# Expert affinities as fp32 products of an fp32 x^T, weights spread on VectorE, x split on GpSimd

## The chip, the core and the metric

One core of a Trainium2 chip runs the whole program. The metric is device time in microseconds (us), the median of several runs: lower is better. The engines are PE (TensorE), DVE (VectorE), ACT (ScalarE), POOL (GpSimd) and SP (the queue that issues the DMAs).

## The reference

The input is eight sequences of 512 tokens by 128 values. Three steps follow each other, each of them normalising its input over the 128 values first:

```
x = x + 0.5 * ffn(layernorm(x))          # first FFN
x = x + attn(layernorm(x))               # a gated step: two 128x128 products, a shift by one token, a sigmoid gate
x = x + 0.5 * ffn(layernorm(x))          # second FFN, same weights

def ffn(x):                              # x: tokens x 128
    shared = silu(x @ Ws_up) @ Ws_down
    aff = x @ centroids.T                # tokens x 64 experts
    idx = top_k(aff + expert_biases, 8)
    w = sigmoid(aff[idx]); w = w / (sum(w) + 1e-8)
    cw = w scattered to tokens x 64, zero elsewhere
    y = sum over experts e of cw[:, e] * (silu(x @ W_up[e]) @ W_down[e])      # 64 experts, 128 -> 64 -> 128
    return shared + y
```

All experts are computed for all tokens, and `cw` weighs them.

## The kernel before

The program works through 16 phases. A phase is one FFN of one sequence: 33 tiles of 512 tokens, tile 0 the shared expert and 32 tiles of two hidden columns of all 64 experts. Each tile has an up product into one of five PSUM banks `up`, a silu in place (ACT, L421), a product with the routing weights `cw` (DVE, L580; tile 0 has none), a split of the result into `g_hi` (fp32r, ACT, L429) and `g_lo` (the rest: even tiles DVE L589, odd tiles POOL L353), and a down product that adds into the bank `y_ps`. Up and down products are each three matmuls, hi*hi, lo*hi and hi*lo (L711 to L713). In its queue PE has the down product of tile t-6 ahead of the up product of tile t, and before tile t it waits until tile t-5 has been taken out of its bank.

Beside these tiles, at slots t given by tables (`AT_FIRST` for the first phase, `AT_SECOND`, `AT_THIRD`, then `AT_STEADY_A` and `AT_STEADY_B` in a loop of five turns, `AT_MID_PREP` and `AT_LAST`), each engine does a piece of the rest. Every engine walks the slots in the same order, so a table's number sets the place in its queue. The routing of the next phase is such a piece:

- PE turns the normalised `normed` to x^T in the PSUM bank `side1` (`x_t`, L720). ACT rounds it to `x_hi` (L408), DVE takes the rest as `x_lo` (L533).
- PE multiplies x_hi with `ce_both` (the centroids, hi and lo side by side, L731) and x_lo with the hi half (L732), four pairs, into `side1`. DVE adds the two halves to `aff` (L537), ACT takes the sigmoid (L412), DVE adds the bias (L541), finds the eight largest (L547), marks them (L554), selects (L561), sums (L566), adds 1e-8 (L570) and inverts (L574).
- POOL multiplies and doubles to `w_dup` (L347), PE turns it (L720), ACT copies it to `cw` (L416). In the first phase w_dup is made on DVE (L692).

The other pieces are the two layernorms around the attention (DVE L513, L520, L526, POOL L341, L343), the attention's products (L752 to L757) and its end on DVE: `t1` (L646) and `x2` (L656). Sigmoid and silu each load their table on ACT (1.28 us).

Before the first phase a prologue loads and norms the first sequence and goes through its routing, while PE runs fill-in products (`keep_busy`, L707). The weights come in four DMA pieces and are split hi/lo in eight pieces of each kind: hi on ACT (L478, L483), lo on DVE (L595) or POOL (L360, L367).

Of the kernel before, what the change touches and what calls it, by code (L numbers as in the profile page):

```python
# [6 lines left out]
B, T, D = 8, 512, 128  # L7
# [27 lines left out]
WARM_START, WARM_ROWS, WARM_ROUTE = 12, 4, 7  # L35
# [3 lines left out]
class Phase:  # L39
# [22 lines left out]
    "x_t": 11, "x_hi": 12, "x_lo": 12, "aff": 16, "aff_sum": 16, "sig": 18, "bias": 17, "max": 18, "take": 18,  # L62
    "gate": 20, "sum": 22, "eps": 23, "inv": 24, "cw": 25, "cw_t": 33, "cw_copy": 33,
# [24 lines left out]
    "x_t": 6, "x_hi": 7, "x_lo": 9, "aff": 12, "aff_sum": 12, "sig": 15, "bias": 13, "max": 15, "take": 15,  # L88
    "gate": 17, "sum": 20, "eps": 22, "inv": 23, "cw": 24, "cw_t": 31, "cw_copy": 32,
# [41 lines left out]
def build(nc, x, ident_in, cent_t, ebias, ws_up, ws_down, w_up, w_down, wb, wb_t, wbf, wbf_t, w1, w2, b_in, out):  # L131
# [3 lines left out]
    with ctx:  # L135
# [20 lines left out]
        ce_both = sb("ce_both", [P, 2 * E], fp32r)  # L156
# [6 lines left out]

        x_hi = [sb(f"x_hi{q}", [P, T], fp32r) for q in range(2)]
# [724 lines left out]
```

## Time and profile before

| what | value |
|---|---|
| median of 3 runs | 822.33 us (821.82 to 822.52) |
| the profiled execution | 821.78 us, its span 820.0 us |
| PE busy | 805.1 us, 98% |
| DVE, ACT, POOL busy | 692.7, 650.7, 408.3 us |
| granted TensorE clock | full in all 40 slices |

The span runs from the first to the last instruction; the 1.8 us around it belong to the time too. PE's busy time is the union of its matmuls, which overlap; how densely they follow each other is read from their starts. The DMAs matter in the first 20 us alone (slices 1 and 2: 267 and 23 GB/s).

### The profile page before, as it was taken

What the parts mean: (1) busy time and instruction counts of PE and PEld (TensorE: products, weight loads), DVE (VectorE), ACT (ScalarE), POOL (GpSimd) and SP (SyncE); (2) the same over time, 40 slices, a digit from 0 to 9 for tenths busy, and PEclk for the clock granted to TensorE, in tenths of its full rate; (3) what the DMA queues carried; (4) which work ended last, traced back from release to release, by engine and by line L of the source; (5) the groups of instructions that cost most, each with busy time, mean ns of one, the idle gap of its engine ahead of it and who ended that gap; (6) DMA issues with size and microseconds to landing.
All of it is one profiled execution on the core that took longest, in us unless ns stands there. A gap on an engine that the chain in (4) does not pass through costs nothing.

```text
span 820.0 us, 12468 instructions
## 1 busy us (share of the span) xinstructions
PE 805.1 (98%) x3691; PEld 649.5 (79%) x3691; DVE 692.7 (84%) x1451; ACT 650.7 (79%) x1204; POOL 408.3 (50%) x360
## 2 busy tenths in 40 slices
PE   7999999999999999999999999999999999999998
PEld 5778878778888788888888788887888878888786
DVE  7987989888798887988879888798897988788875
ACT  5897778778787787877878688886888868786975
POOL 2884545545455453544535445364463644554453
PEclk9999999999999999999999999999999999999999
DMA  7000000000000000000000000000000000000000
GB/s 267 23 0 14 14 1 1 1 10 17 14 1 0 21 4 13 0 0 26 0 13 0 0 26 0 13 0 0 26 0 0 0 1 27 0 1 1 14 0 14
DMA packets 16046, 11.51 MB, mean 14 GB/s; under 512 B 1680, under 2 KB 14992, under 8 KB 16016
## 3 DMA queue, kind: packets, MB, share of 16 engines
q1 hardware_dynamic: 16016, 11.15, 4.4%
q8 instruction: 15, 0.25, 0.1%
q14 instruction: 15, 0.12, 0.1%
HBM read 9.05 MB, written 2.10 MB: 14 GB/s over the span
## 4 chain that ended last, share of the span: by engine, by line
PE 77%; DVE 14%; ACT 5%; issue 1%; POOL 1%; DMA 0%; DVEq 0%; ACTq 0%; POOLq 0%
PE up L711 12%; PE up L712 12%; PE up L713 12%; PE y_ps L711 11%; PE y_ps L713 11%; PE y_ps L712 11%; PE side L720 3%; DVE x L656 3%; DVE g_lo L589 2%; DVE gated L580 2%; ACT up L421 2%; ACT g_hi L429 2%; DVE normed L526 2%; DVE up L580 2%; PE side L731 1%
## 5 line engine op out<-in xcount | busy, mean ns | idle before, releaser
L353 POOL TENSOR_TENSOR g_lo<-gated,g_hi 128x512 fp32r<-128x512 f32 x256 | 331.9, 1297 | 372.5 <-ACT g_hi L429 372.5
L421 ACT ACTIVATE up<-up 128x512 f32<-128x512 f32 x528 | 310.7, 590 | 73.6 <-PE up L713 72.1
L580 DVE TENSOR_TENSOR gated<-up,cw 128x512 f32<-128x512 f32 x256 | 175.3, 685 | 58.1 <-ACT up L421 53.9
L711 PE MATMUL y_ps<-g_hi,wd_hi 128*128 128x512 f32 x512 | 208.0, 406 | 1.8 <-POOL g_lo L353 1.7
L711 PE MATMUL up<-x_hi,wu_hi 128*128 128x512 f32 x512 | 203.1, 397 | 1.8 <-DVE g_lo L589 1.8
L713 PE MATMUL y_ps<-g_hi,wd_lo 128*128 128x512 f32 x512 | 202.5, 396 | 0.0
L712 PE MATMUL up<-x_lo,wu_hi 128*128 128x512 f32 x512 | 202.3, 395 | 0.0
L713 PE MATMUL up<-x_hi,wu_lo 128*128 128x512 f32 x512 | 201.7, 394 | 0.0
L712 PE MATMUL y_ps<-g_lo,wd_hi 128*128 128x512 f32 x512 | 201.6, 394 | 0.0
L429 ACT CAST g_hi<-up 128x512 fp32r<-128x512 f32 x272 | 161.2, 592 | 47.8 <-DVE up L580 45.8
L580 DVE TENSOR_TENSOR up<-up,cw 128x512 f32<-128x512 f32 x256 | 176.4, 689 | 18.1 <-ACT up L421 14.4
L589 DVE TENSOR_TENSOR g_lo<-up,g_hi 128x512 fp32r<-128x512 f32 x256 | 174.3, 681 | 10.6 <-ACT g_hi L429 9.3
L429 ACT CAST g_hi<-gated 128x512 fp32r<-128x512 f32 x256 | 157.4, 615 | 28.8 <-DVE gated L580 26.8
L711 PEld LDWEIGHTS up<-x_hi,wu_hi 128*128 128x128 f32 x512 | 96.3, 188 | 27.3 <-DVE g_lo L589 4.1
L711 PEld LDWEIGHTS y_ps<-g_hi,wd_hi 128*128 128x128 f32 x512 | 96.4, 188 | 25.1 <-POOL g_lo L353 4.1
L713 PEld LDWEIGHTS y_ps<-g_hi,wd_lo 128*128 128x128 f32 x512 | 96.3, 188 | 23.0
L713 PEld LDWEIGHTS up<-x_hi,wu_lo 128*128 128x128 f32 x512 | 96.3, 188 | 22.5
L712 PEld LDWEIGHTS up<-x_lo,wu_hi 128*128 128x128 f32 x512 | 96.4, 188 | 22.3
L712 PEld LDWEIGHTS y_ps<-g_lo,wd_hi 128*128 128x128 f32 x512 | 96.6, 189 | 18.7
L526 DVE TENSOR_SCALAR normed<-x,mv,rstd 128x128 f32<-128x128 f32 x64 | 35.0, 598 | 1.3 <-POOL rstd L343 1.1
L589 DVE TENSOR_TENSOR g_hi<-up,g_hi 64x512 fp32r<-64x512 f32 x16 | 11.1, 694 | 20.0 <-ACT g_hi L429 19.8
L343 POOL TENSOR_TENSOR rstd<-var_eps,neg_half 128x4 f32<-128x4 f32 x24 | 25.3, 1053 | 2.0
(101 smaller groups left out, 570.9 us busy)
## 6 DMA issues: line engine op xcount, KB each, us to landing
x_in<-in_x SPq DMA_DIRECT2D x8, 256.0 KB, 2.8
wu_raw<-in_w_up SPq DMA_DIRECT2D x4, 512.0 KB, 6.1
wd_raw<-in_w_down SPq DMA_DIRECT2D x4, 512.0 KB, 7.0
x_res<-in_x SPq DMA_DIRECT2D x8, 256.0 KB, 2.8
out<-out_sb SPq DMA_DIRECT2D x7, 256.0 KB, 2.2
out<-out_sb SPq DMA_DIRECT2D x2, 128.0 KB, 1.9
sm_raw<-in_ident SPq DMA_DIRECT2D x2, 64.0 KB, 5.4
ident<-in_ident SPq DMA_DIRECT2D x1, 64.0 KB, 2.2
```

Source lines behind the costliest of these rows:

```text
L343: nc.gpsimd.tensor_tensor(rstd[k][:, :], var_eps[k][:, :], neg_half[:, :], ALU.pow).then_inc(rstd_done[k], 1)
L353: nc.gpsimd.tensor_tensor(g_lo[:, i, :], gated[:, t // 2 % ORING, :], g_hi[:, i, :].bitcast(fp32), ALU.subtract).then_inc(lo_done[1], 1)
L421: nc.scalar.activation(up[i][:, :], up[i][:, :], ACT.Silu).then_inc(silu_done, 1)
L429: nc.scalar.copy(g_hi[:, t % GRING, :], src).then_inc(hi_done, 1)
L526: made = nc.vector.tensor_scalar(normed[k][:, n, :], norm_from[k][:, n, :], mv[k][:, n, 0:1], rstd[k][:, n:n + 1], ALU.subtract, ALU.mult)
L580: nc.vector.tensor_tensor(gated[:, t // 2 % ORING, :] if t % 2 else up[i][:, :], up[i][:, :], cw[ph.q][:, :], ALU.mult).then_inc(gate_done, 1)
L589: nc.vector.tensor_tensor(lo[ps, i, :], up[t % RING][ps, :], g_hi[ps, i, :].bitcast(fp32), ALU.subtract).then_inc(lo_done[0], 1)
L656: made = nc.vector.scalar_tensor_tensor(x2[:, m, :], t1[:, m, :], gamma[:, m:m + 1], xu[:, m, :], ALU.mult, ALU.add)
L711: nc.tensor.matmul(o, a[0], b[0], start=start, stop=False)
L712: nc.tensor.matmul(o, a[0], b[1], start=False, stop=False)
L713: return nc.tensor.matmul(o, a[1], b[0], start=False, stop=stop)
L720: last = nc.tensor.transpose(rows(dst, n), src(n), ident[:, :])
```

## The change

- Affinities: ACT copies x^T unrounded to a new fp32 tile `x_raw`, and PE multiplies it with the fp32 centroids in four products of 64 columns. `ce_both`, its split and the sum of the halves (L537) are gone. `aff` is now a view of `side1`: the bias is added and the sigmoid taken from PSUM, and the sigmoid waits for the bias add.
- The hi and lo of x come from `x_raw`, both on POOL (on DVE for the first x).
- `w_dup` is made on DVE right behind the inversion. The 1e-8 stands in a 65th column of `w_sel`, so that its addition is gone.
- `t1` is written back to the attention's PSUM tile, and `x2` reads it there.
- Prologue: the first x is normed, turned and copied in two halves; `sm_lo` and the first piece of `wu_lo` move to POOL; 3 fill-in products in place of 4 and 3 in place of 7.
- The tables move the routing two to eight slots ahead, and the attention's products one.

```diff
-WARM_START, WARM_ROWS, WARM_ROUTE = 12, 4, 7
+WARM_START, WARM_ROWS, WARM_ROUTE = 12, 3, 3
 AT_FIRST = {
-    "x_t": 11, "x_hi": 12, "x_lo": 12, "aff": 16, "aff_sum": 16, "sig": 18, "bias": 17, "max": 18, "take": 18,
-    "gate": 20, "sum": 22, "eps": 23, "inv": 24, "cw": 25, "cw_t": 33, "cw_copy": 33,
+    "x_t": 11, "x_copy": 11, "x_split": 13, "aff": 14, "sig": 17, "bias": 15, "max": 17, "take": 17,
+    "gate": 18, "sum": 21, "inv": 22, "cw_t": 33, "cw_copy": 33,
...
+        aff = side1.rearrange("p (n d) -> p n d", n=NB)[:, :, 0:E]
...
-            def spread(q, n):
-                pool.wait_ge(inv_done[q], n + 1)
-                nc.gpsimd.tensor_tensor(*spread_operands, ALU.mult).then_inc(dup_done[q], 1)
+            def x_split(q, n):
+                hold(pool, x_copied[q], n + 1)
+                nc.gpsimd.tensor_copy(x_hi[q][:, :], x_raw[:, :]).then_inc(x_hi_done[q], 1)
+                pool.wait_ge(x_hi_done[q], n + 1)
+                nc.gpsimd.tensor_tensor(x_lo[q][:, :], x_raw[:, :], x_hi[q][:, :].bitcast(fp32),
+                                        ALU.subtract).then_inc(x_lo_done[q], 1)
...
             rstd_of(0, 0)
+            pool.wait_ge(sm_hi_done, 1)
+            nc.gpsimd.tensor_tensor(sm_lo[:, :], sm_raw[:, 0:A1], sm_hi[:, :].bitcast(fp32), ALU.subtract).then_inc(sm_lo_done, 1)
+            split_up(0)
             split_up(1)
...
-            def x_high(q, n):
+            def x_copy(q, n):
                 act.wait_ge(x_turned[q], n + 1)
-                nc.scalar.copy(x_hi[q][:, :], side1).then_inc(x_hi_done[q], 1)
+                nc.scalar.copy(x_raw[:, :], side1).then_inc(x_copied[q], 1)

             def sigmoid(q, n):
-                act.wait_ge(aff_summed[q], n + 1)
-                nc.scalar.activation(sig[:, :, :], aff[:, :, :], ACT.Sigmoid).then_inc(sig_done[q], 1)
+                act.wait_ge(bias_done[q], n + 1)
+                nc.scalar.activation(sig[:, :, :], aff, ACT.Sigmoid).then_inc(sig_done[q], 1)
...
-            x_high(0, 0)
+            act.wait_ge(half_turned, 1)
+            nc.scalar.copy(x_raw[:, half(0, T)], side0[:, half(0, T)])
+            act.wait_ge(x_turned[0], 1)
+            nc.scalar.copy(x_raw[:, half(1, T)], side1[:, half(1, T)]).then_inc(x_copied[0], 1)
...
             def affinities(q, n):
-                pe.wait_ge(x_lo_done[q], n + 1)
-
+                pe.wait_ge(x_copied[q], n + 1)
                 for m in range(NB):
-                    nc.tensor.matmul(rows(side1, m), rows(x_hi[q], m), ce_both[:, :], start=True, stop=False)
-                    last = nc.tensor.matmul(side1[:, m * P:m * P + E], rows(x_lo[q], m), ce_both[:, 0:E], start=False, stop=True)
+                    last = nc.tensor.matmul(aff[:, m, :], rows(x_raw, m), ce_raw[:, :], start=True, stop=True)
                 last.then_inc(aff_done[q], 1)
...
-                        nc.vector.tensor_tensor(t1[:, :, :], att[:, :, 0:D], normed[1][:, :, :],
+                        nc.vector.tensor_tensor(att[:, :, 0:D], att[:, :, 0:D], normed[1][:, :, :],
                                                 ALU.subtract).then_inc(t1_done, 1)
...
+            def spread(q, n):
+                dve.wait_ge(inv_done[q], n + 1)
+                nc.vector.tensor_tensor(*spread_operands, ALU.mult).then_inc(dup_done[q], 1)
...
+            nc.vector.memset(w_sel[:, :, E:E + 1], SUM_EPS)
+            norm(0, 0, range(0, NB // 2), False, half_normed)
+            norm(0, 0, range(NB // 2, NB))
+            dve.wait_ge(x_copied[0], 1)
+            nc.vector.tensor_copy(x_hi[0][:, :], x_raw[:, :]).then_inc(x_hi_done[0], 1)
+            dve.wait_ge(x_hi_done[0], 1)
+            nc.vector.tensor_tensor(x_lo[0][:, :], x_raw[:, :], x_hi[0][:, :].bitcast(fp32), ALU.subtract).then_inc(x_lo_done[0], 1)
```

The order on DVE in the prologue, from the last norm to the first w_dup. Before:

```order
L526 TENSOR_SCALAR normed0<-x_in,mv0,rstd0 128x128 x3
L677 TENSOR_TENSOR ce_both<-ce_raw,ce_both 128x64 [waits ce_hi_done]
L533 TENSOR_TENSOR x_lo0<-side,x_hi0 128x512 [waits x_hi_done0]
L681 TENSOR_TENSOR sm_lo<-sm_raw,sm_hi 128x256 [waits sm_hi_done]
L595 TENSOR_TENSOR wu_lo<-wu_raw,wu_hi 128x512 [waits wu_hi_done]
L537 TENSOR_REDUCE aff<-side 128x256 [waits aff_done0]
L541 TENSOR_TENSOR biased<-aff,bias_b 128x256 [waits aff_summed0]
```

Now, on the same engine and stretch:

```order
L536 TENSOR_SCALAR normed0<-x_in,mv0,rstd0 128x128
L683 CAST x_hi0<-x_raw 128x512 [waits x_copied0]
L685 TENSOR_TENSOR x_lo0<-x_raw,x_hi0 128x512 [waits x_hi_done0]
L545 TENSOR_TENSOR biased<-side,bias_b 128x256 [waits aff_done0]
```

Three splits and the sum have left DVE's queue, and one cast has come.

The order on POOL in the first phase, slots 11 to 16 (`g_lo` there is an odd tile's, `wd_lo` and `wu_lo` are weight pieces). Before:

```order
L360 TENSOR_TENSOR wu_lo<-wu_raw,wu_hi 128x512 [waits wu_hi_done]
L353 TENSOR_TENSOR g_lo<-gated,g_hi 128x512 [waits hi_done]
L367 TENSOR_TENSOR wd_lo<-wd_raw,wd_hi 128x512 [waits wd_hi_done]
L353 TENSOR_TENSOR g_lo<-gated,g_hi 128x512 [waits hi_done]
L367 TENSOR_TENSOR wd_lo<-wd_raw,wd_hi 128x512 [waits wd_hi_done]
```

Now:

```order
L365 TENSOR_TENSOR wu_lo<-wu_raw,wu_hi 128x512 [waits wu_hi_done]
L358 TENSOR_TENSOR g_lo<-gated,g_hi 128x512 [waits hi_done]
L372 TENSOR_TENSOR wd_lo<-wd_raw,wd_hi 128x512 [waits wd_hi_done]
L349 CAST x_hi1<-x_raw 128x512 [waits x_copied1]
L351 TENSOR_TENSOR x_lo1<-x_raw,x_hi1 128x512 [waits x_hi_done1]
L358 TENSOR_TENSOR g_lo<-gated,g_hi 128x512 [waits hi_done]
L372 TENSOR_TENSOR wd_lo<-wd_raw,wd_hi 128x512 [waits wd_hi_done]
```

The two instructions of the split stand ahead of the `g_lo` of tile 13.

The order on DVE at the end of the last phase but one, where the last routing is made. Before:

```order
L554 MATCH_REPLACE taken<-top,biased 128x64 [waits top_done1]
L554 MATCH_REPLACE taken<-top,biased 128x64 x3
L561 SCALAR_TENSOR_TENSOR w_sel<-taken,sig 128x256 [waits taken_done1,sig_done1]
L589 TENSOR_TENSOR g_lo<-up2,g_hi 128x512 [waits hi_done]
L566 TENSOR_REDUCE w_sum<-w_sel 128x4 [waits sel_done1]
L570 TENSOR_SCALAR w_eps<-w_sum 128x4 [waits sum_done1]
L574 RECIPROCAL w_inv<-w_eps 128x4 [waits sum_eps_done1]
L589 TENSOR_TENSOR g_hi<-up0,g_hi 64x512 [waits hi_done]
```

Now:

```order
L565 SCALAR_TENSOR_TENSOR w_sel<-taken,sig 128x4x64 [waits taken_done1,sig_done1]
L570 TENSOR_REDUCE w_sum<-w_sel 128x4 [waits sel_done1]
L584 TENSOR_TENSOR up2<-up2,cw0 128x512 [waits silu_done]
L574 RECIPROCAL w_inv<-w_sum 128x4 [waits sum_done1]
L578 TENSOR_TENSOR w_dup<-w_sel,w_inv 128x512 [waits inv_done1]
L593 TENSOR_TENSOR g_lo<-up2,g_hi 128x512 [waits hi_done]
L593 TENSOR_TENSOR g_hi<-up0,g_hi 64x512 [waits hi_done]
```

Selection and sum now stand ahead of the gating of tile 32, and w_dup ahead of the last `g_lo` and on this engine.

## Rows read from the trace of the kernel before

**Rows 1.** The page, part 1: busy us, share and instructions of each engine.

```profile
PE 805.1 (98%) x3691; PEld 649.5 (79%) x3691; DVE 692.7 (84%) x1451; ACT 650.7 (79%) x1204; POOL 408.3 (50%) x360
```

**Rows 2.** Busy time by stretch: length, PE, PEld, DVE, ACT, POOL busy, clock, DMA.

```profile
28.00:46.00 18.00, 17.73 (x85) 14.74 (x86) 15.55 (x37) 17.31 (x32) 14.55 (x11) 1.00 0.05 16
120.00:760.00 640.00, 637.99 (x2945) 516.87 (x2944) 548.55 (x1136) 513.07 (x952) 315.29 (x276) 1.00 0.02 7
```

**Rows 3.** Timeline of 0 to 20 us: start, length, engine, line, operation.

```profile
8.37 0.59 ACT L408 CAST x_hi<-side 128x512 fp32r<-128x512 f32 x1 [0.78 <-PE side L720]
...
9.46 1.14 ACT L478 CAST wu_hi<-wu_raw 128x512 fp32r<-128x512 f32 x2 [0.51 <-DMA wu_raw<-in_w_up]
...
10.68 1.30 POOL L360 TENSOR_TENSOR wu_lo<-wu_raw,wu_hi 128x512 fp32r<-128x512 f32 x1 [4.28 <-ACT wu_hi L478]
...
10.72 0.62 ACT L483 CAST wd_hi<-wd_raw 128x512 fp32r<-128x512 f32 x1
...
11.63 0.42 ACT L412 ACTIVATE sig<-aff 128x256 f32<-128x256 f32 x1 [0.29 <-DVE aff L537]
11.64 0.63 DVE L541 TENSOR_TENSOR biased<-aff,bias_b 128x256 f32<-128x256 f32 x1
...
13.92 0.43 DVE L561 SCALAR_TENSOR_TENSOR w_sel<-taken,sig 128x256 f32<-128x256 f32 x1
...
14.81 1.11 ACT L421 ACTIVATE up<-up 128x512 f32<-128x512 f32 x2
...
15.25 0.69 DVE L692 TENSOR_TENSOR w_dup<-w_sel,w_inv 128x512 f32<-128x512 f32 x1
...
15.99 0.66 PE L720 MATMUL side<-ident,w_dup 128*128 128x128 f32 x4 [0.64 <-DVE w_dup L692]
...
16.69 0.59 ACT L416 COPY cw<-side 128x512 f32<-128x512 f32 x1 [0.77 <-PE side L720]
```

**Rows 4.** PE's timeline: three small groups of products, each with the row behind it.

```profile
29.06 0.28 PE L818 MATMUL side<-sm_raw,wb_sb 128*128 128x2 f32 x2
...
29.43 0.63 PE L720 MATMUL side<-ident,normed 128*128 128x128 f32 x4
...
36.87 0.22 PE L731 MATMUL side<-ce_both,x_hi 128*128 128x128 f32 x1
...
37.68 0.48 PE L711 MATMUL y_ps<-g_hi,wd_hi 128*128 128x512 f32 x1
...
88.10 0.38 PE L752 MATMUL side<-sm_raw,u_mid 128*128 128x130 f32 x2
...
90.25 0.48 PE L711 MATMUL y_ps<-g_hi,wd_hi 128*128 128x512 f32 x1
```

**Rows 5.** PE's timeline: the waits at the seams after the prologue.

```profile
50.94 0.48 PE L711 MATMUL up<-x_hi,wu_hi 128*128 128x512 f32 x1 [0.61 <-DVE g_lo L589]
...
104.95 0.66 PE L720 MATMUL side<-ident,normed 128*128 128x128 f32 x4 [0.50 <-DVE normed L526]
...
118.94 0.50 PE L711 MATMUL up<-x_hi,wu_hi 128*128 128x512 f32 x1 [0.59 <-DVE g_lo L589]
...
770.20 0.66 PE L720 MATMUL side<-ident,w_dup 128*128 128x128 f32 x4 [0.65 <-POOL w_dup L347]
```

**Rows 6.** Durations of one line: ns least/median/most, first and last start.

```profile
L541 DVE TENSOR_TENSOR biased<-aff,bias_b x16: 415/876/1237, 11.6 to 764.7; 128x256 f32<-128x256 f32 x16
```

**Rows 7.** Groups by line and shape: busy us, mean ns; two of POOL's.

```profile
L347 POOL TENSOR_TENSOR w_dup<-w_sel,w_inv 128x512 f32<-128x512 f32 x15 | 15.6, 1041 | 6.8 <-DVE w_inv L574 6.8
...
L393 POOL COPY x_kept<-x 128x512 f32<-128x512 f32 x8 | 4.9, 612 | 0.0
```

**Rows 8.** Timeline of 37 to 50 us: POOL's g_lo, PE's use, a select.

```profile
37.97 1.32 POOL L353 TENSOR_TENSOR g_lo<-gated,g_hi 128x512 fp32r<-128x512 f32 x1
...
40.54 0.40 PE L711 MATMUL y_ps<-g_hi,wd_hi 128*128 128x512 f32 x1
...
48.04 1.55 DVE L561 SCALAR_TENSOR_TENSOR w_sel<-taken,sig 128x256 f32<-128x256 f32 x1
```

More of the change, by code:

```diff
@@ L87 @@
 AT_STEADY_A = {
-    "x_t": 6, "x_hi": 7, "x_lo": 9, "aff": 12, "aff_sum": 12, "sig": 15, "bias": 13, "max": 15, "take": 15,
-    "gate": 17, "sum": 20, "eps": 22, "inv": 23, "cw": 24, "cw_t": 31, "cw_copy": 32,
+    "x_t": 6, "x_copy": 6, "x_split": 9, "aff": 10, "sig": 13, "bias": 11, "max": 13, "take": 13,
+    "gate": 14, "sum": 16, "inv": 18, "cw_t": 26, "cw_copy": 26,
     "y_t": 6,
@@ L94 @@
 AT_STEADY_B = {
-    "x_t": 1, "x_hi": 2, "x_lo": 4, "aff": 7, "aff_sum": 7, "sig": 9, "bias": 8, "max": 9, "take": 9,
-    "gate": 11, "sum": 14, "eps": 15, "inv": 17, "cw": 18, "cw_t": 23, "cw_copy": 23,
+    "x_t": 1, "x_copy": 1, "x_split": 3, "aff": 6, "sig": 8, "bias": 7, "max": 8, "take": 8,
+    "gate": 9, "sum": 11, "inv": 13, "cw_t": 18, "cw_copy": 18,
     "y_t": 6, "x1": 8, "stat1": (10, 12), "aggr1": 13, "rstd1": 14, "norm1": (16, 18), "xu": 19, "u_t": 22,
-    "u_copy": 22, "attn": 26, "tanh": 26, "gamma": 26, "t1": 26, "x2": (28, 29),
-    "stat2": (30, 31), "aggr2": 31, "rstd2": 32, "norm2": (33, 34),
+    "u_copy": 22, "attn": 25, "tanh": 25, "gamma": 25, "t1": 25, "x2": (27, 28),
+    "stat2": (29, 30), "aggr2": 30, "rstd2": 31, "norm2": (33, 34),
     "y": 2,
@@ L102 @@
 AT_MID_PREP = {
-    "x_t": 27, "x_hi": 27, "x_lo": 27, "aff": 31, "aff_sum": 31, "sig": 32, "bias": 31, "max": 31, "take": 32,
-    "gate": 32, "sum": 33, "eps": 33, "inv": 33, "cw": 33,
-    "y_t": 5, "x1": 6, "stat1": (7, 7), "aggr1": 8, "rstd1": 8, "norm1": (9, 10), "xu": 10, "u_t": 14,
+    "x_t": 27, "x_copy": 27, "x_split": 28, "aff": 29, "sig": 30, "bias": 29, "max": 30, "take": 30,
+    "gate": 31, "sum": 31, "inv": 32,
+    "y_t": 5, "x1": 6, "stat1": (7, 7), "aggr1": 8, "rstd1": 8, "norm1": (9, 10), "xu": 11, "u_t": 14,
     "u_copy": 14, "attn": 17, "tanh": 18, "gamma": 16, "t1": 18, "x2": (19, 19),
@@ L161, in build @@
         neg_half = sb("neg_half", [P, NB])
+        x_raw = sb("x_raw", [P, T])
         x_hi = [sb(f"x_hi{q}", [P, T], fp32r) for q in range(2)]
@@ L521, in aggr, with norm @@
                 last.then_inc(mv_done[k], 1)
-            def norm(k, c, blocks=range(NB), last=True):
+            def norm(k, c, blocks=range(NB), last=True, part=None):
                 dve.wait_ge(rstd_done[k], c + 1)
@@ L633, in phase @@
                             norm(k, c, blocks, last)
-                    for name, step in (("x_lo", x_low), ("aff_sum", sum_aff), ("bias", add_bias), ("max", find_top), ("take", take_top),
-                                       ("gate", select), ("sum", sum_up), ("eps", add_eps), ("inv", invert)):
+                    for name, step in (("bias", add_bias), ("max", find_top), ("take", take_top), ("gate", select), ("sum", sum_up), ("inv", invert),
+                                       ("inv", spread)):
                         if ph.at.get(name) == t:
@@ L846, in _ @@
             pe.wait_ge(consts_set, 1)
-            keep_busy(WARM_START, side0, zeros_r[:, :], g_hi[:, 0, :])
+            keep_busy(WARM_START, y_ps[:, :], zeros_r[:, :], g_hi[:, 0, :])
             pe.wait_ge(small_in[0], 48)
-            turn_x(0, 0, 0, 0)
-            keep_busy(WARM_ROWS, side0, zeros_r[:, :], g_hi[:, 0, :])
-            pe.wait_ge(ce_lo_done, 1)
+            for h in range(2):
+                if h == 0:
+                    pe.wait_ge(half_normed, 1)
+                else:
+                    pe.wait_ge(norm_done[0], 1)
+                for m in range(h * NB // 2, (h + 1) * NB // 2):
+                    last = nc.tensor.transpose(rows((side0, side1)[h], m), normed[0][:, m, :], ident[:, :])
+                last.then_inc(half_turned if h == 0 else x_turned[0], 1)
+            keep_busy(WARM_ROWS, y_ps[:, :], zeros_r[:, :], g_hi[:, 0, :])
             affinities(0, 0)
```

92 lines of the change are left out of this document (36 added, 56 removed).

## The prediction, made before the changed kernel was run

> **What bounds the kernel now.** I read the page's busy times first, then busy time by stretch, then PE's timeline for its gaps, then the other engines' timelines at those gaps. PE is busy for 805.1 of 820.0 us [rows 1], and from 120 to 760 us for 637.99 of 640.00, while no other engine passes 549 us there [rows 2]. So PE's own stream of matmuls sets the time in that stretch: what DVE, ACT or POOL save there is worth nothing, and what they lose costs nothing until a wait reaches PE. What can be won lies in three kinds of places. (a) The prologue: the tiles that need the routing cannot go on until its weights are copied, which starts at 16.69 us [rows 3]. (b) The seams between phases, where PE waits for DVE or POOL for 0.50 to 0.65 us each [rows 5]. (c) PE's own small products, if they become shorter. In the first phase ACT is nearly full, 17.31 of 18 us, and POOL has 14.55 [rows 2]: there a slower step can reach PE.
>
> **The affinities on PE.** Before: eight products per routing, from 36.87 to 37.68 us, 0.81 us or 0.101 each [rows 4]. After: four fp32 products of 64 columns. The rows show what fp32 products do: those of the v vector (2 columns) stand as x2 for each instruction, and the four records, 29.06 to 29.43, take 0.093 each; the attention's (130 columns, ten instructions, 20 records) take 88.10 to 90.25, 0.107 each [rows 4]. So four instructions are eight records of 0.093 to 0.107 us: 0.74 to 0.86 us per routing, against 0.81. Over 16 routings that is -1.1 to +0.8 us; I take 0, as 64 columns lie between.
>
> **The prologue.** Two chains meet at the copy to `cw`.
> - ACT's own. It casts the first weight pieces from 9.46 us, which waits for the DMA and doesn't move; the last of them ends at 10.72+0.62 = 11.34. The sigmoid then waited 0.29 us for the sum of the halves, to 11.63 [rows 3]. Now it waits for the bias add instead. That ends early enough (next point), so the sigmoid, the table load and the four silus come 0.29 us earlier, and the last pair ends at 14.81+1.11-0.29 = 15.63.
> - The routing's. The second half of the first x is normed when the whole was, but only two blocks are turned and half the columns copied behind it (0.42 us, as the sigmoid of 256 columns, for 0.59), and two turns fewer stand ahead: the copy ends at about 8.55 against 8.37+0.59 = 8.96. On DVE comes the cast to x_hi, which no row shows: I bound it by nothing less than half of a 512-column two-input op, 0.35, and the whole of it, 0.69 (the w_dup row), and take 0.6, nearer to the row. With x_lo (0.69) DVE is free at 9.85. PE's affinities, which wait for the copy alone, are done by then. The bias add, 0.42 us (below), ends at 10.3, against 11.64+0.63 = 12.27. From there to the start of w_dup took 15.25-12.27 = 2.98 us; I keep it, though the addition of 1e-8 is gone. But POOL now has both first pieces of wu_lo, 2 x 1.30 us from about 10.05 (half of the cast from 9.46) to 12.65, and the select, which began 13.92-12.27 = 1.65 behind the add and is due at 11.95 now, may have to wait for them (see the lock below): 0.7 more. So w_dup runs 14.0 to 14.7 and the turn starts at 14.75, where it started at 15.99, and is over at 15.4.
> - So ACT is late next: the copy starts at 15.63, not 16.69: -1.06 us. PE's fill-in products lie before the turn either way. The bounds: if nothing but ACT's 0.29 is passed on, -0.3; if ACT's silus aren't last, the turn's own gain, 1.24.
>
> All that stands behind the copy in the first phase (gating, g_hi, g_lo on POOL, PE's first down products) is a chain that starts at it, so it shifts as a whole.
>
> **The first phase.** POOL gets the split of x ahead of the g_lo of tile 13: a one-input copy, 0.61 [rows 7], and a two-input op of 1.30 [rows 3], 1.91 us. POOL is without a pause there; it ended that g_lo at 37.97+1.32 = 39.29, PE took it at 40.54 [rows 8], 1.25 us of slack. So PE waits about 0.7 us. Later in the phase PE waits anyway, as at 50.94 for 0.61 [rows 5], on a chain of DVE and ACT that a late PE doesn't lengthen, so about half is given back: +0.3, bounds 0 and +0.7. DVE loses x_lo, the sum and the 1e-8 and gets w_dup, 0.69: it is not worse off.
>
> **The lock.** The bias add has two SBUF inputs and took 415 ns at best, 876 in the median and 1237 at most [rows 6]; the select, also two, took 0.43 at 13.92 [rows 3] and 1.55 at 48.04 [rows 8]. So such an op on DVE can be held up by about the length of a POOL op, 1.30 us. The bias add now reads one input from PSUM, and x2 as well: I take 0.42 for the add. w_dup, new on DVE, has two SBUF inputs: 0.69 us, and up to 1.30 before it. The Trainium skill (SBUF — State Buffer, section "Who interferes with whom") says the same of both: one SBUF input doesn't contend, two do with a GpSimd op that reads SBUF, and the second to issue fully blocks. By that rule the change trades some of these waits for others; it speaks against w_dup on DVE and is the third rival below.
>
> **The seams.** At 104.95 PE waited 0.50 us for the norm behind x2, at 118.94 0.59 us for a g_lo of DVE behind a bias add and two table loads, and at 770.20 0.65 us for w_dup on POOL [rows 5]. The norm's chain is the shorter by x2's blocked time, the second loses the sum of the halves and most of the add's wait, and the third has 0.69 in place of POOL's 1.04 [rows 7], loses the addition, and comes from affinities two slots earlier. I take all three as gone: -1.74. In their place the table loads now fall two slots earlier, while PE still runs both products per slot; I leave that to the range.
>
> **In the steady loop** POOL has 315.29 of 640 us of work [rows 2]; per routing it gets 1.91 and gives 1.04 [rows 7]: no wait. I take 0.
>
> **The sum.** -1.06 +0.3 -1.74 + 0 = -2.5 us, against the profiled execution's 821.78 (span 820.0 and 1.8 around it): 819.3. The median of the runs shown, 822.33, is 0.55 above that execution; so 819.8 as a median. The bounds of the terms together: from -1.24-1.1-1.74 = -4.1 to -0.3+0.8+0.7 = +1.2 with no seam gained.
>
> **The rivals.**
> 1. The seams stay: other waits of the same size take their place (the earlier table loads, PE arriving earlier at the same late op). For it: both table loads stay, and DVE's queue holds nearly the same work around them. Against it: the routing's chain is shorter by more than the waits. Then -1.06+0.3 = -0.8: 821.5.
> 2. More goes: the first phase's waits too (0.61 at 50.94 and about as much around it), and the seam before the last phase but one, as the bias add and x_lo are off DVE. For it: the wait at 50.94 stands right behind the blocked select. Against: the select can be blocked again. Then -2.5-1.2-0.3 (no loss at tile 13) and a little from the prologue: 818.0.
> 3. Slower: w_dup on DVE waits for POOL, up to 1.30+0.69 = 2 us in one piece, and the gating of the tiles stands behind it; the gating waits, ACT's g_hi with it, and PE finds its bank not free. The price is the wait that followed the one select of 1.55: 0.61 [rows 5, 8]. There are 15 such w_dup; the gains of 2.5 are used up at four, and from seven on the kernel is slower by more than can be told from no change. At ten it is +6.1-2.5 = +3.6: 825.9. Against it: in 120 to 760 us the bias adds were blocked as long, and PE lost 2 us in all of 640 [rows 2].
>
> That the change doesn't do what it says isn't to be expected: the order shows each step moved.
>
> **How the numbers follow.** Forecast 0.48, rival 1 0.22, rival 2 0.18, rival 3 0.12. About 0.2%, 1.6 us, is what a measurement of this kernel can tell from no change; so faster means below 820.7. The forecast (two thirds of it and more below, some of it within 0.2%) and rival 2 give faster 0.64, rival 1 and the rest of the forecast same 0.24, rival 3 slower 0.12. Range: 817.4 takes in rival 2 and its bound, 822.6 rival 1 with the unknown costs on top; rival 3 is left out.
>
> **What would show it.** In the changed profile: eight records per routing in about 0.8 us; the copy to `cw` at 15.6 us with ACT without a pause before it; PE waiting for POOL's g_lo near 40 us; no wait of PE at the turns of the norm in the second phase and of the last w_dup; w_dup rows on DVE between 0.69 and 2.0. The forecast is wrong if PE's busy share of the long stretch falls (rival 3), if the affinity records are longer than 0.107, or if the table loads bring a new wait at the seams (rival 1).

## The result, and the profile after

The changed kernel takes 824.89 us (median of 7 runs, 824.67 to 825.05), the kernel before 821.82 (7 runs beside it, 821.73 to 822.52): a ratio of 1.0035, interval 1.0023 to 1.0047, 3.1 us slower. Forecast were 819.8, in a range of 817.4 to 822.6. Of the signs that the prediction named against itself, two came: PE's busy share of the long stretch fell (rival 3's sign), and the table loads brought a new wait at the seams (rival 1's).

Busy times and stretches after, from the page and from the view of busy time by stretch (the latter: length, then PE, PEld, DVE, ACT, POOL):

```profile
PE 805.7 (98%) x3686; PEld 649.3 (79%) x3686; DVE 666.2 (81%) x1418; ACT 652.1 (79%) x1204; POOL 424.8 (52%) x377
```

```profile
28.00:46.00 18.00, 16.91 (x80) 13.71 (x80) 14.16 (x34) 17.25 (x31) 15.16 (x13) 1.00 0.00 1
120.00:760.00 640.00, 635.93 (x2933) 515.03 (x2932) 525.18 (x1107) 511.15 (x945) 325.69 (x287) 1.00 0.02 7
```

DVE has lost 26.5 us of work [rows 1] and PE yet has 2.06 us less busy time in the long stretch than before [rows 2]: PE waits more. Where, the first up product of each phase tells (`up<-x_hi,sm_hi` in PE's timeline, 16 of them). The distance from one to the next is a phase's length. First kind and second kind are the two phases of a turn of the loop (`AT_STEADY_A`, `AT_STEADY_B`).

| us | before | after | difference |
|---|---|---|---|
| start of the first phase | 10.71 | 10.24 | -0.47 |
| phase 0 | 53.71 | 53.32 | -0.39 |
| phase 1 | 50.97 | 51.85 | +0.88 |
| phase 2 (`AT_THIRD`) | 53.43 | 52.26 | -1.17 |
| six of the first kind, together | 290.61 | 293.45 | +2.84 |
| five of the second kind, together | 255.79 | 256.53 | +0.74 |
| last but one (phase 14) | 50.67 | 51.85 | +1.18 |

What lies behind these phases (phase 15 and the end) is 0.6 us shorter, so the span is 3.0 longer. All phases of one kind look alike, so one of each is enough.

**The prologue.** PE's, DVE's and ACT's timeline after, 8 to 16 us (start, length, engine, line, operation):

```profile
8.94 0.43 DVE L683 CAST x_hi<-x_raw 128x512 fp32r<-128x512 f32 x1 [0.94 <-ACT x_raw L503]
...
9.04 1.03 PE L731 MATMUL side<-ce_raw,x_raw 128*128 128x64 f32 x8
...
10.11 0.42 DVE L545 TENSOR_TENSOR biased<-side,bias_b 128x256 f32<-128x256 f32 x1
...
12.19 0.66 DVE L565 SCALAR_TENSOR_TENSOR w_sel<-taken,sig 128x256 f32<-128x256 f32 x1
...
14.26 1.10 ACT L430 ACTIVATE up<-up 128x512 f32<-128x512 f32 x2
14.31 0.66 PE L721 MATMUL side<-ident,w_dup 128*128 128x128 f32 x4
...
15.25 0.62 ACT L425 COPY cw<-side 128x512 f32<-128x512 f32 x1
```

These answer to [rows 3]. The copy to `cw` starts at 15.25, not 16.69. The turn of w_dup is over by 14.97, and ACT goes on from its last silus (14.26+1.10 = 15.36, the two rows overlap) to the copy without a pause: ACT is the last to be ready, as forecast.

**A phase of the loop's first kind.** ACT's, POOL's, DVE's and PE's timeline after, 187 to 196 us:

```profile
187.95 1.28 ACT L421 ACT_TABLE_LOAD   x1
...
189.65 1.28 ACT L430 ACT_TABLE_LOAD   x1
...
191.56 0.70 DVE L584 TENSOR_TENSOR up<-up,cw 128x512 f32<-128x512 f32 x1 [1.27 <-ACT up L430]
...
192.12 1.29 POOL L358 TENSOR_TENSOR g_lo<-gated,g_hi 128x512 fp32r<-128x512 f32 x1 [4.19 <-ACT g_hi L438]
...
192.56 1.14 DVE L565 SCALAR_TENSOR_TENSOR w_sel<-taken,sig 128x256 f32<-128x256 f32 x1
...
193.62 0.68 DVE L584 TENSOR_TENSOR gated<-up,cw 128x512 f32<-128x512 f32 x1
194.23 0.67 DVE L593 TENSOR_TENSOR g_lo<-up,g_hi 128x512 fp32r<-128x512 f32 x1
...
194.96 0.50 PE L712 MATMUL up<-x_hi,wu_hi 128*128 128x512 f32 x1 [0.47 <-DVE g_lo L593]
```

Read it upward from the last row. PE waits for a `g_lo`, that for a gating, and that stood behind the select. The select took 1.14 us: it began while POOL's `g_lo` (192.12 to 193.41) was running and ended behind it. Before it DVE had been 1.27 us idle, because ACT was loading the sigmoid's and the silu's tables. So two delays lie in one place: the table loads make ACT and DVE late, and the select, now three slots nearer to them, comes before DVE has caught up. (PE's waits as the profile shows them in brackets are some 0.17 us shorter than the gap in PE's starts, since matmuls overlap; the gap here is 0.64.)

**The seam to phase 2.** The same view, 110 to 116 us:

```profile
110.37 1.28 ACT L421 ACT_TABLE_LOAD   x1
...
112.07 1.28 ACT L430 ACT_TABLE_LOAD   x1
...
113.98 0.69 DVE L584 TENSOR_TENSOR gated<-up,cw 128x512 f32<-128x512 f32 x1 [2.01 <-ACT up L430]
...
115.41 0.47 PE L712 MATMUL up<-x_hi,sm_hi 128*128 128x512 f32 x1 [1.32 <-DVE g_lo L593]
```

The old waits of [rows 5] at 104.95 and 118.94 are gone; this new one is larger than both. It stands at 769.50 too, in place of the one at 770.20.

**What the prediction had overlooked in the kernel before.** It took [rows 2] (PE busy for 637.99 of 640 us) to mean that nothing was to be gained there. DVE, POOL and PE before, 261 to 269 us, the end of a phase of the second kind:

```profile
261.78 1.29 POOL L353 TENSOR_TENSOR g_lo<-gated,g_hi 128x512 fp32r<-128x512 f32 x1 [3.02 <-ACT g_hi L429]
...
261.82 1.67 DVE L656 SCALAR_TENSOR_TENSOR x<-t,gamma,xu 128x128 f32<-128x128 f32 x2
...
264.61 1.65 DVE L656 SCALAR_TENSOR_TENSOR x<-t,gamma,xu 128x128 f32<-128x128 f32 x2
...
268.49 0.50 PE L711 MATMUL up<-x_hi,sm_hi 128*128 128x512 f32 x1 [0.23 <-DVE g_lo L589]
```

A phase has four x2, in two pairs, and here each pair meets a `g_lo` of POOL and holds DVE for 1.67 and 1.65 us; in the median an x2 takes 0.35:

```profile
L656 DVE SCALAR_TENSOR_TENSOR x<-t,gamma,xu x32: 334/346/1409, 95.5 to 746.8; 128x128 f32<-128x128 f32 x32
```

The gap in PE's starts at 268.49 is 0.40 us (0.63 from start to start, of which 0.23 are the usual distance). Such a gap stands at the end of six phases, and each has a tail: the product behind it takes 0.50 in place of 0.39 to 0.40 and the next one starts 0.10 us late.

### The profile page after: what moved, and what is told of

Same layout as the page of the kernel before. It is cut to its first block, busy times and chain, and to the rows that moved or that the text cites. A ratio compares the mean times of both kernels' runs of the same rounds, so it can differ in the third digit from the quotient of the medians.

```text
span 823.0 us, 12451 instructions
## 1 busy us (share of the span) xinstructions
PE 805.7 (98%) x3686; PEld 649.3 (79%) x3686; DVE 666.2 (81%) x1418; ACT 652.1 (79%) x1204; POOL 424.8 (52%) x377
## 4 chain that ended last, share of the span: by engine, by line
PE 73%; DVE 10%; ACT 8%; issue 6%; POOL 1%; DMA 1%; SPq 1%; DVEq 0%; ACTq 0%
PE up L712 12%; PE up L714 11%; PE up L713 11%; PE y_ps L712 11%; PE y_ps L714 11%; PE y_ps L713 11%; ACT L430 2%; PE side L721 2%; DVE gated L584 2%; ACT up L430 2%; DVE g_lo L593 2%; DVE up L584 2%; ACT g_hi L438 2%; PE side L731 1%; ACT L421 1%
## 5 line engine op out<-in xcount | busy, mean ns | idle before, releaser
L712 PE MATMUL up<-x_hi,wu_hi 128*128 128x512 f32 x512 | 205.5, 401 | 4.6 <-DVE g_lo L593 3.7
L536 DVE TENSOR_SCALAR normed<-x,mv,rstd 128x128 f32<-128x128 f32 x64 | 31.7, 545 | 1.2 <-POOL rstd L345 1.2
```

The source lines that it names most:

```text
L536: made = nc.vector.tensor_scalar(normed[k][:, n, :], norm_from[k][:, n, :], mv[k][:, n, 0:1], rstd[k][:, n:n + 1], ALU.subtract, ALU.mult)
L712: nc.tensor.matmul(o, a[0], b[0], start=start, stop=False)
```

## The experiments

Each kernel ran beside the kernel before, whose median was 821.78, 821.84 and 821.97 us in the three groups of runs (e1 to e4, e5 to e8, e9 and e10). What was measured:

| | us (range) | ratio to before (interval) |
|---|---|---|
| changed kernel | 824.89 (824.67 to 825.05) | 1.0035 (1.0023 to 1.0047) |
| e1 | 819.76 (819.48 to 820.13) | 0.9975 (0.9965 to 0.9985) |
| e2 | 822.14 (821.80 to 822.32) | 1.0004 (0.9994 to 1.0013) |
| e3 | 824.01 (823.91 to 824.32) | 1.0027 (1.0016 to 1.0038) |
| e4 | 812.69 (812.31 to 812.82) | 0.9887 (0.9871 to 0.9904) |
| e5 | 822.06 (821.92 to 822.16) | 1.0003 (0.9993 to 1.0012) |
| e6 | 852.95 (852.38 to 854.68) | 1.0382 (1.0364 to 1.0399) |
| e7 | 818.59 (818.20 to 818.94) | 0.9959 (0.9945 to 0.9973) |
| e8 | 812.54 (812.21 to 812.81) | 0.9884 (0.9868 to 0.9901) |
| e9 | 813.19 (813.00 to 813.22) | 0.9893 (0.9878 to 0.9908) |
| e10 | 815.19 (815.11 to 815.28) | 0.9917 (0.9904 to 0.9931) |

### e1: the select later in the loop's first kind

```diff
 AT_STEADY_A = {
-    "gate": 14, "sum": 16, "inv": 18, "cw_t": 26, "cw_copy": 26,
+    "gate": 17, "sum": 18, "inv": 20, "cw_t": 26, "cw_copy": 26,
```

> Changed kernel, only the select, sum and inversion of the first kind of loop phase moved back from slots 14, 16, 18 to 17, 18, 20. Theory T (placement): in each of the six or seven phases of this kind PE waits 0.64 us for a g_lo of DVE, because the select, held up by POOL's g_lo (1.14 us), stands ahead of the gating that has to catch up after the two table loads. Moved back, these waits go: about 0.49 us each in six phases, 824.9 to about 822.0. Theory W (w_dup on VectorE is the cost, by its lock): the w_dup's wait stays wherever the select stands, no more than 0.5 us gained, 824.4 or above. Theory P (GpSimd's split of x is the cost): nothing changes, 824.9.

It gave 5.1 us. Select and its neighbours on DVE, 191 to 197 us:

```profile
191.70 0.70 DVE L584 TENSOR_TENSOR up<-up,cw 128x512 f32<-128x512 f32 x1 [1.27 <-ACT up L430]
...
195.97 0.41 DVE L565 SCALAR_TENSOR_TENSOR w_sel<-taken,sig 128x256 f32<-128x256 f32 x1
```

DVE's 1.27 us behind the tables are still there, and now cost nothing: the select starts 4.3 us behind that gating, where it was 1.0, takes 0.41, and PE doesn't wait. The edit moves w_dup two slots as well; that one is still held up (1.32 us at 199.23, 1.46 in the changed kernel). These phases are 48.08 us long in place of 48.9. That is 0.84 less on average, more than the 0.64 of the gap itself: its tail of 0.10 went too, and with it a second small wait of 0.07 at 200.72 with a tail of its own.

### e2: the last routing of the two seams where it was

```diff
 AT_SECOND = {        # the same in AT_MID_PREP
-    ... "aff": 29, "sig": 30, "bias": 29, "max": 30, "take": 30,
-    "gate": 31, "sum": 31, "inv": 32,
+    ... "aff": 31, "sig": 32, "bias": 31, "max": 31, "take": 32,
+    "gate": 33, "sum": 33, "inv": 33,
```

> Changed kernel, only the last part of the routing in the second phase and in the last but one put back to where it stood before (affinities and bias add in slot 31, sigmoid 32, select, sum, inversion 33). Theory T: the two waits of 1.5 us at PE's first product of the following phase (115.41 and 769.5 us) come from the table loads in slots 30 and 31, ahead of the gating of tiles whose banks the next phase needs; they go, and waits of 0.7 to 0.8 us, as before the change, come back in each place: 824.9 to about 823.4. Theories W and P: the waits stay at 1.5, or shift, no gain: 824.9; if the shorter path to w_dup was worth something, it is slower by up to 1.5.

It gave 2.75 us. Phases 1 and 14 take 50.29 us each, 1.56 less; the waits at 115.41 and 769.50 are gone, and one of 0.39 for w_dup at 770.10 has come. The edit moves the whole end of the routing; that it is the table loads which made both waits is read from the rows of 110 to 116 us, where DVE waits 2.01 us for ACT's silu behind them. With the sigmoid at slot 32 the first load (112.98) falls where PE has only down products left (its last up product began by 111.43), the second (115.15) behind the first products of the next phase, and PE has no wait.

### e3: w_dup on POOL again

```diff
-                dve.wait_ge(inv_done[q], n + 1)
-                nc.vector.tensor_tensor(*spread_operands, ALU.mult).then_inc(dup_done[q], 1)
+                pool.wait_ge(inv_done[q], n + 1)
+                nc.gpsimd.tensor_tensor(*spread_operands, ALU.mult).then_inc(dup_done[q], 1)
```

> Changed kernel, only w_dup back on GpSimd, at the slot of the inversion. Theory T: the select's waits and the seams stay; only the small waits of the second kind of loop phase (0.3 us and some tenths of restarts, behind a w_dup of 1.6 us) go, 0.2 to 0.4 us in each of six: 824.9 to about 823.2. Theory W: the w_dup on VectorE (median 1.46 us) is what costs, in the first kind of phase too: 3 us or more gained, 821.9 or below. Theory P: nothing or slower, as GpSimd gets 1.04 more per routing: 825 or above.

It gave 0.9 us (the POOL instruction stands at the same slot). The phases of the second kind are 0.3 us shorter, but in phase 2 PE waits 1.28 us for w_dup (at 144.36), and the waits of 0.64 and 1.5 stay. So w_dup on DVE, my third rival, accounts for 0.9 of the 3.1 us. Behind that net sum lies more: the loop's phases are 2.5 us shorter with w_dup on POOL (1.0 in the first kind, 1.5 in the second), phase 2 is 1.3 and phase 0 0.4 longer.

### e4: the change's operations with the tables of before

All slots that both kernels have got the numbers of before (the split of x stays at its own). A part of it:

```diff
 AT_STEADY_A = {
-    "x_copy": 6, "aff": 10, "sig": 13, "bias": 11, "max": 13, "gate": 14, "sum": 16, "inv": 18, "cw_t": 26, "cw_copy": 26,
+    "x_copy": 7, "aff": 12, "sig": 15, "bias": 13, "max": 15, "gate": 17, "sum": 20, "inv": 23, "cw_t": 31, "cw_copy": 32,
 AT_STEADY_B = {
-    "gate": 9, "sum": 11, "inv": 13, "attn": 25, "tanh": 25, "x2": (27, 28), "stat2": (29, 30),
+    "gate": 11, "sum": 14, "inv": 17, "attn": 26, "tanh": 26, "x2": (28, 29), "stat2": (30, 31),
```

> Changed kernel with all operations of the change, but every slot of the tables that the change moved put back to its old number (the split of x on GpSimd, which has no old slot, stays). Theory T: the cost of the change lies in the slots alone; the gains of the prologue (-0.5 in the profile at PE's first product, about as much in the first phase) and of the shorter steps stay: below the kernel before, 820.5 to 821.3. Theory W or P (an operation itself costs): it stays slower than before, 823 or above.

812.69 us: 12.2 less than the changed kernel and 9.1 less than before. The cause was named rightly, but its size was again too small. The same stretch as in [rows 2], and two groups of lines (ns least/median/most):

```profile
120.00:760.00 640.00, 639.95 (x2972) 523.55 (x2970) 522.53 (x1131) 517.61 (x958) 335.17 (x292) 1.00 0.02 7
```

```profile
L578 DVE TENSOR_TENSOR w_dup<-w_sel,w_inv x15: 691/692/1166, 52.8 to 760.3; 128x512 f32<-128x512 f32 x15
```

```profile
L565 DVE SCALAR_TENSOR_TENSOR w_sel<-taken,sig x16: 393/415/1545, 12.3 to 758.6; 128x256 f32<-128x256 f32 x16
```

PE is busy for 639.95 of 640 us, and in its starts no phase of the loop's turns has a gap for a wait. The same two groups in the changed kernel:

```profile
L578 DVE TENSOR_TENSOR w_dup<-w_sel,w_inv x15: 691/1458/1603, 50.2 to 770.9; 128x512 f32<-128x512 f32 x15
```

```profile
L565 DVE SCALAR_TENSOR_TENSOR w_sel<-taken,sig x16: 412/896/1541, 12.2 to 769.3; 128x256 f32<-128x256 f32 x16
```

In the median w_dup takes 1.46 us at slots 13 and 18 and 0.69 at 17 and 23: whether it meets POOL's `g_lo` is a matter of the slot. The seam, 112 to 116 us, for comparison with the one above:

```profile
112.04 1.28 ACT L421 ACT_TABLE_LOAD   x1
...
113.70 0.39 PE L712 MATMUL up<-x_hi,sm_hi 128*128 128x512 f32 x1
...
114.75 1.28 ACT L430 ACT_TABLE_LOAD   x1
```

### e5: the routing alone put back, in the second kind

```diff
 AT_STEADY_B = {
-    "gate": 9, "sum": 11, "inv": 13, "cw_t": 18, "cw_copy": 18,
+    "gate": 11, "sum": 14, "inv": 17, "cw_t": 23, "cw_copy": 23,
```

> The changed kernel, with one table alone altered: in STEADY_B (second-kind phases of the loop) the rest of the routing goes back to its old slots (selection 9 to 11, sum 11 to 14, inversion and w_dup 13 to 17, turn and copy 18 to 23); the attention's slots stay one earlier, as changed. Theory T1: the waits in these phases come because the select and w_dup, each up to 1.6 us under the lock, stand close together and right ahead of the two halves of the norm (slots 16 and 18); apart from each other they cost nothing: about 0.5 us less in each of the 6 phases, 3 us in all, 821.8. Rival R1: the attention's products and x2, one slot earlier, cause them: no change, 824.9, phases of the second kind stay at 51.3 us.

822.06: 2.8 us less, as T1 has it for the sum. Of its two ops only w_dup was held up: in the changed kernel's phases of this kind the select takes 0.41 to 0.42 us, w_dup 1.59 to 1.60; here w_dup takes 0.69. The phases take 50.77 us, as in e4, so the attention's slots, one earlier, cost nothing. In the changed kernel a w_dup at 240.18 took 1.60 us beside POOL's `g_lo` and ACT's `g_hi` then waited 2.07 us for DVE.

### e6: the old operations with the new slots

```diff
 AT_STEADY_A = {      # in the kernel before; so in all tables
-    "x_t": 6, "x_hi": 7, "x_lo": 9, "aff": 12, "aff_sum": 12, "sig": 15, "bias": 13, "max": 15, "take": 15,
-    "gate": 17, "sum": 20, "eps": 22, "inv": 23, "cw": 24, "cw_t": 31, "cw_copy": 32,
+    "x_t": 6, "x_hi": 6, "x_lo": 9, "aff": 10, "aff_sum": 10, "sig": 13, "bias": 11, "max": 13, "take": 13,
+    "gate": 14, "sum": 16, "eps": 17, "inv": 18, "cw": 18, "cw_t": 26, "cw_copy": 26,
```

> The kernel before with its own operations, but with the changed kernel's slot numbers in all tables. Theory T2: the numbers cost time whatever the operations are, since they put the two table loads and the select where DVE and ACT are late already: waits of some 0.5 us or more in each phase of the loop's first kind and 1 us or more at the two seams, 826 or above. Rival R2: the numbers hurt the new operations alone (w_dup on DVE, the sigmoid behind the bias add): 822, as before.

852.95: the numbers cost the old operations 31 us, far more than the 4 expected. The page's group of the first affinity product, and two rows of DVE and PE:

```profile
L731 PE MATMUL side<-ce_both,x_hi 128*128 128x128 f32 x64 | 16.3, 315 | 19.3 <-DVE x_lo L533 19.3
```

```profile
195.07 0.68 DVE L533 TENSOR_TENSOR x_lo<-side,x_hi 128x512 fp32r<-128x512 f32 x1
...
195.80 0.33 PE L731 MATMUL side<-ce_both,x_hi 128*128 128x128 f32 x1 [1.30 <-DVE x_lo L533]
```

19.3 us of idle time of PE are its wait for x_lo, which the old affinities need and the new ones don't. So this run carries a wait of its own and can't price the numbers for the new operations. It shows that they cost in both. An x_lo at an earlier slot wasn't tried, so whether the old operations could take an earlier routing stays open. The other 12 us weren't taken apart; a part of them is a lower clock (last section).

### e7: t1 in SBUF again, in e4

```diff
-                        nc.vector.tensor_tensor(att[:, :, 0:D], att[:, :, 0:D], normed[1][:, :, :],
+                        nc.vector.tensor_tensor(t1[:, :, :], att[:, :, 0:D], normed[1][:, :, :],
-    ... scalar_tensor_tensor(x2[:, m, :], att[:, m, 0:D], gamma[:, m:m + 1], xu[:, m, :], ...
+    ... scalar_tensor_tensor(x2[:, m, :], t1[:, m, :], gamma[:, m:m + 1], xu[:, m, :], ...
```

> The version with the new operations and the old slots (812.7 us), with one part of the change undone: t1 goes to a tile in SBUF again, so that x2 has two inputs in SBUF. Theory T3: PE's wait at the end of each second-kind phase of the loop, 0.4 us six times in the kernel before, came from x2 held up by POOL's g_lo (1.67 us in place of 0.60); it comes back: about +2.5 us, 815.2. Rival R3: it went because DVE has less to do in all (no x_lo, no sum of halves): no change, 812.7.

818.59: +5.9 us. T3 holds, at more than twice its size. DVE, POOL and PE, 159 to 174 us, the end of phase 2 and what follows:

```profile
159.76 1.67 DVE L660 SCALAR_TENSOR_TENSOR x<-t,gamma,xu 128x128 f32<-128x128 f32 x2
...
162.56 1.65 DVE L660 SCALAR_TENSOR_TENSOR x<-t,gamma,xu 128x128 f32<-128x128 f32 x2
...
166.44 0.51 PE L712 MATMUL up<-x_hi,sm_hi 128*128 128x512 f32 x1 [0.26 <-DVE g_lo L593]
...
173.05 0.51 PE L773 MATMUL y_ps<-g_hi,sm_hi 128*128 128x512 f32 x1
```

Held x2 cost PE four times: a gap of 0.42 at 166.44, its tail of 0.10, a second gap of 0.22 at 173.05 (the norm behind x2 is late, and, as I read it, the shared expert's product with it) and its tail of 0.10. That is 0.8 for a pair of phases, of which the expectation had the first alone. A gap of 0.61 at 103.81 in phase 1 is back besides.

### e8: the split of x later in the first phase, in e4

```diff
 AT_FIRST = {
-    "x_t": 11, "x_copy": 12, "x_split": 13, ...
+    "x_t": 11, "x_copy": 12, "x_split": 18, ...
```

> The version with the new operations and the old slots (812.7 us), with the split of x in the first phase (AT_FIRST) moved from slot 13 to 18, behind three more of POOL's own pieces. Theory T4: PE's wait of 0.79 us at 40.31, for the g_lo of tile 13 behind that split, goes and nothing follows: 811.9. Rival R4: POOL is full there and the wait only moves to a later g_lo: 812.7.

812.54, no difference. The gap of 0.79 at 40.31 is gone; the ones behind it have grown:

```profile
45.92 0.50 PE L712 MATMUL up<-x_hi,wu_hi 128*128 128x512 f32 x1 [0.22 <-DVE g_lo L593]
...
49.58 0.47 PE L712 MATMUL up<-x_hi,wu_hi 128*128 128x512 f32 x1 [0.60 <-DVE g_lo L593]
```

Gaps of 0.39 and 0.77 stand where e4 had one of 0.37. R4 holds in that nothing is won (0.79+0.37 and 0.39+0.77 are the same 1.16), though the wait moved to DVE's `g_lo`, not to one of POOL's.

### e9: w_dup on POOL, in e4

```diff
-                nc.vector.tensor_tensor(*spread_operands, ALU.mult).then_inc(dup_done[q], 1)
+                nc.gpsimd.tensor_tensor(*spread_operands, ALU.mult).then_inc(dup_done[q], 1)
```

> The version with the new operations and the old slots (812.7 us), with w_dup on POOL again, at the same slot. Theory T5: with those slots w_dup is hardly held up on DVE (691 ns in the median) and hides on either engine; on POOL it is some 0.4 us longer and comes late only in the last phase but one, where the kernel before waited 0.65 us for it: about +0.6, 813.3. Rival R5: w_dup on DVE is what the good time rests on (POOL then has both the split and w_dup, 3.2 us per routing, and its g_lo come late in each phase): +3 us or more, 816.

813.19: +0.5 us, and +0.3 when each is set against the kernel before of its own group (821.97 and 821.78). That is within what the two intervals allow, so T5's +0.6 can't be told from nothing; R5's +3 is excluded. Every phase of the loop stays as in e4 (48.04 and 50.70), and PE waits 0.33 us for w_dup at 761.02.

### e10: t1 in PSUM alone, in the kernel before

```diff
-                        nc.vector.tensor_tensor(t1[:, :, :], att[:, :, 0:D], normed[1][:, :, :],
+                        nc.vector.tensor_tensor(att[:, :, 0:D], att[:, :, 0:D], normed[1][:, :, :],
-    ... scalar_tensor_tensor(x2[:, m, :], t1[:, m, :], gamma[:, m:m + 1], xu[:, m, :], ...
+    ... scalar_tensor_tensor(x2[:, m, :], att[:, m, 0:D], gamma[:, m:m + 1], xu[:, m, :], ...
-                            pe.wait_ge(t1_done, ph.norm2 + 1)
+                            pe.wait_ge(x2_done, ph.norm2 + 1)
```

> The kernel before with one part of the change alone: t1 written back to the attention's PSUM tile and x2 read from there. Theory T6: the 5.9 us that this part was worth among the new operations are its own (x2 no longer held up by POOL's g_lo, in seven phases of either kind): 816 to 817. Rival R6: without the rest of the change DVE still has x_lo and the sum of the halves, and only the wait of 0.4 us at the end of six phases and the one of 0.67 at 104.95 go: about -3, 818.9.

815.19: 6.8 us less than before, 0.8 more than T6 has; R6 is out. x2 again, and the start of the next phase, for comparison with the rows of 261 to 269 us above:

```profile
259.89 1.30 POOL L353 TENSOR_TENSOR g_lo<-gated,g_hi 128x512 fp32r<-128x512 f32 x1 [3.01 <-ACT g_hi L429]
259.92 0.60 DVE L656 SCALAR_TENSOR_TENSOR x<-side,gamma,xu 128x128 f32<-128x128 f32 x2
...
266.17 0.40 PE L711 MATMUL up<-x_hi,sm_hi 128*128 128x512 f32 x1
```

The same op meets the same `g_lo` and takes 0.60, not 1.67, because one input comes from PSUM. This part of a long change carries three quarters of what its operations bring with the old slots (6.8 of 9.1 us).

## Why the prediction was wrong

Two terms of the sum failed: the steady loop, taken as 0, and the seams, taken as -1.74 with the earlier table loads at nothing. The slots cost the loop about 8 us and the seams 2.8, while t1 in PSUM brought the loop 4.5.

The account of the 3.1 us from these runs, each set against the kernel before of its own group: t1 in PSUM -6.8 (e10); the rest of the operations, the prologue among them, -2.3 (e4's -9.1 less e10's -6.8); the new slots +12.2 (changed kernel less e4). By e7 t1 is worth 5.8 and the rest 3.3, so the two shares are known to about 1 us. Of the 12.2, 5.1 are the first kind's select and what was moved with it (e1), 2.8 the seams (e2), 2.8 the second kind's routing (e5); 1.5 are left. The traces place them: phases 0 and 2 are 0.3 and 0.5 us shorter in e4, the first kind 0.2 in all below e1, and e2's wait of 0.39 for w_dup isn't there. No run was made for these alone.

- **The prologue** (taken -1.06): right, and more. The copy to `cw` starts 1.44 us earlier, behind ACT's silus as forecast; these moved by 0.55, not 0.29, while the turn of w_dup moved by 1.68. The first phase ends 0.86 us earlier (63.56 for 64.42), where prologue and first phase together were taken as -0.76. The cast to x_hi took 0.43, not 0.6, and the select 0.66, so it was held up by 0.25 and not 0.7.
- **The affinities** (taken 0): right. Eight records, from their start at 32.68 to that of the next product at 33.48, take 0.80 us, where it was 0.81 [rows 4]; in the phases behind it is 0.80 to 0.84, and 0.88 and 0.89 in phases 1 and 14, where the bound was 0.86:

```profile
32.68 1.00 PE L731 MATMUL side<-ce_raw,x_raw 128*128 128x64 f32 x8
...
33.48 0.48 PE L712 MATMUL y_ps<-g_hi,wd_hi 128*128 128x512 f32 x1
```

- **The first phase** (+0.3): the wait at tile 13 came, 1.09 us by the profile at 40.40 where 0.7 was expected, and in e8, where it is avoided, nothing is gained: with the old slots around it, the place of the split costs about 0. That a wait here is given back was right, even more than assumed.
- **The seams** (-1.74): this step failed. The three waits named went. But the sentence "the table loads now fall two slots earlier ... I leave that to the range" passed over two waits of 1.5 us. What it needed was one sum: two loads of 1.28 us stop ACT's silus, and with them DVE and the bank that PE needs, while PE asks for two products per slot. From the first load at 110.37 to the next silu at 113.36 ACT made none for 2.99 us.
- **The steady loop** (0): the step that failed most, in both directions. From PE's busy share I concluded that nothing was to be gained, and from POOL's work that no wait would come. The loop's phases gained 4.5 of e10's 6.8 us, and the slots cost them about 8 (e1 and e5). I had weighed what POOL has to do, and not where in DVE's queue the select and w_dup come to stand.
- **The lock** was read rightly as a thing (an op with two SBUF inputs is held up for as long as a POOL op) and applied in part only: to w_dup (third rival) and to x2 at the seam, but not to x2 in the loop, whose length in the stretch of [rows 2] I hadn't looked up. The Trainium skill's rule (SBUF — State Buffer, "Who interferes with whom": one SBUF input doesn't contend, two do with a GpSimd op that reads SBUF) agrees with e10: a pair of x2 takes 1.67 us with two, 0.60 with one.
- The first rival (other waits take the seams' place) was right in mechanism; it was priced as equal to the old ones and is larger.
- The third rival gave 825.9, near the 824.9 measured, and that is luck: w_dup on DVE is worth 0.9 us of it (e3). Its mechanism is there in the loop, where w_dup takes 1.46 and 1.60 us in the new slots; in the old ones it takes 0.69 and costs nothing (e4, e9). It is the slot that sets whether it is held up.

Not tried: the first phase with its old slots alone, phase 2 alone, and in e1 and e2 the pieces that were moved together one by one.

## What to carry to other kernels

A busy share of 99.7% (637.99 of 640 us) hid 0.8 us of gaps per pair of phases, since matmuls overlap: read the gaps from the starts, and the longest against the least time of each line there, before calling a stretch worth nothing. In a software pipeline the slot of an instruction is an operation of its own with a price: try new operations with the old slots and the new slots apart, for here the one was worth -9.1 and the other +12.2 us. Where DVE shares a stretch with a POOL that streams from SBUF, each DVE op with two SBUF inputs whose longest time stands far above its least (x2: 1409 and 334 ns) is a candidate for a PSUM operand.

## What the runs showed of the hardware

- The norm, a `TENSOR_SCALAR` with one large SBUF input, is held up as well as ops with two: 331 ns least, 1342 most in the kernel before, and 1.49 us for two beside a `g_lo` at 244.24 in the changed one, where the shortest pair takes 0.59. x2 with one input from PSUM isn't: 332 to 344 ns in 32 (e4). The Trainium skill (SBUF — State Buffer, "Who interferes with whom") names such an op among those that can take the shared ports in a fast mode, which agrees. The row of the kernel before:

```profile
L526 DVE TENSOR_SCALAR normed<-x_in,mv,rstd x32: 331/344/1342, 6.4 to 613.2; 128x128 f32<-128x128 f32 x32
```

- In e6 PE stood idle for x_lo three times for over 2 us: 3.36 us ahead of 37.50, 2.09 ahead of 115.26 and 2.09 ahead of 787.82. Each time PE began again at the full clock, and 0.5 to 1.2 us later the granted clock fell to the lower of its two levels (0.50, 1.2 GHz): from 38.0 to 41.1, 116.5 to 119.6 and 788.9 to 792.3 us. Products of 512 columns then began 0.43 us apart in place of 0.23. The first of the three in two stretches, whose 0.60 and 0.65 are means over both levels:

```profile
37.50:40.00 2.50, 2.50 (x11) 2.31 (x12) 1.43 (x5) 0.08 (x1) 2.50 (x3) 0.60 0.00 0
40.00:42.00 2.00, 2.00 (x8) 1.57 (x7) 0.00 (x0) 0.33 (x1) 0.79 (x1) 0.65 0.00 0
```

The clock stayed full behind the waits of 1.5 us in the changed kernel. So each of these three waits cost more than its own length.
- The gaps of PE shown here have a tail: the first product behind one takes 0.47 to 0.51 us, not 0.40, and the second starts 0.07 to 0.11 us late.
